# Token halves for the first and last batch, smaller mask products and a moved residual in a transformer kernel on one core

## What is computed

```python
x = x + L0_xattn(layernorm(x), ctx, ctx)   # 16 heads of width 8, softmax over 77 keys
# two layers on y = layernorm(x):
y = y + local_attention(rotary(l2norm(q), l2norm(k)), v) @ wo    # 8 heads of 64, windows of 64
h = layernorm(shift_token(y)) @ w1 + b1
y = y + (a * gelu(g)) @ w2 + b2                                  # a, g = the halves of h
x = x + y
x = x + softmax(layernorm(x) @ ctx + bias) @ ctx @ w_out         # second cross attention
# last feed-forward on z = layernorm(x), activations rounded to integers:
scale = 127.0 / max(abs(z)); q = clip(round(z * scale), -128.0, 127.0) / scale
x = x + bitlinear(gelu(bitlinear(z)))                            # both products use such rounded q
```

## Time and profile before

| | before |
|---|---|
| median of 3 runs | 757.89 us |
| lowest, highest | 753.37, 759.18 us |
| profiled execution: its time, its span | 759.17, 757.4 us |
| PE busy | 620.7 us, 82% |
| DVE busy | 558.1 us, 74% |
| ACT busy | 441.3 us, 58% |
| POOL busy | 238.4 us, 31% |
| mean granted TensorE clock | 0.934 of full speed |

### The profile page before, as it was taken

How to read it: one execution, slowest core, us unless ns; L and a number is a source line. 1 busy time by engine, 2 the same in 40 slices (tenths; PEclk the granted TensorE clock), 3 DMA queues, 4 the chain that set the end, 5 groups by cost and what they waited for, 6 DMA issues and landing times.

```text
span 757.4 us, 16460 instructions
## 1 busy us (share of the span) xinstructions
PE 620.7 (82%) x6368; PEld 424.3 (56%) x6368; DVE 558.1 (74%) x1344; ACT 441.3 (58%) x1083; POOL 238.4 (31%) x153
## 2 busy tenths in 40 slices
PE   5888877879899987688797899849889998899833
PEld 3565544557555763464564656626557676576621
DVE  3829877795878665855756877688787658979986
ACT  2233413674597668278567578557865963952814
POOL 2001221441224423334345135431443423503420
PEclk9899977998999999899999999959999999999975
DMA  8380001000200010020020020001102000000000
GB/s 223 102 183 1 2 0 37 13 3 2 50 1 2 21 31 1 1 49 1 2 49 1 2 48 2 2 0 29 36 2 49 2 2 1 2 1 15 2 15 14
DMA packets 27993, 19.00 MB, mean 25 GB/s; under 512 B 14894, under 2 KB 23692, under 8 KB 27916
## 3 DMA queue, kind: packets, MB, share of 16 engines
q1 hardware_dynamic: 27196, 17.82, 9.9%
q10 hardware_dynamic: 720, 0.13, 0.1%
HBM read 9.56 MB, written 1.05 MB: 14 GB/s over the span
## 4 chain that ended last, share of the span: by engine, by line
PE 45%; DVE 25%; ACT 14%; issue 8%; SPq 4%; POOL 2%; DMA 1%; DVEq 0%; POOLq 0%; ACTq 0%
PE ps L830 6%; PE ps L759 5%; ACT probs_l L1047 4%; PE ps L895 3%; SPq L571 3%; PE ps L710 3%; PE ps L855 3%; PE ps L867 3%; PE ps L918 3%; PE ps L744 3%; PE ps L842 2%; PE ps L885 2%; ACT squares L1030 2%; DVE rot_b L1358 2%; PE ps L925 2%
## 5 line engine op out<-in xcount | busy, mean ns | idle before, releaser
L650 POOL TENSOR_TENSOR probs_l<-probs_l,row_sum_l 128x1024 f32<-128x1024 f32 x32 | 64.2, 2005 | 130.3 <-DVE row_sum_l L1386 120.6
L643 POOL TENSOR_TENSOR rot_a<-rot_a,rot_b 128x1024 f32<-128x1024 f32 x32 | 76.6, 2398 | 74.4 <-DVE rot_b L1358 74.4
L1047 ACT ACTIVATE probs_l<-ps,neg_max_l 128x128 f32<-128x128 f32 x256 | 90.3, 378 | 13.3 <-DVE neg_max_l L1378 13.1
L830 PE MATMUL ps<-wqkv,hT_l 128*128 128x512 f32 x128 | 72.0, 645 | 17.9 <-DVE rot_b L1358 16.6
L1357 DVE TENSOR_TENSOR rot_a<-ps,rot 128x512 f32<-128x512 f32 x64 | 44.0, 687 | 53.4 <-ACT squares L1030 47.3
L1030 ACT ACTIVATE squares<-ps 128x512 f32<-128x512 f32 x64 | 38.7, 604 | 64.2 <-PE ps L830 62.7
L710 PE MATMUL ps<-k_diag,hT 32*128 32x308 f32 x256 | 57.6, 489 | 13.5 <-DVE probs L1225 8.9
L991 ACT ACTIVATE probsT<-ps 128x512 f32<-128x512 f32 (+1 forms) x96 | 47.7, 528 | 31.2 <-PE ps L744 30.9
L980 ACT ACTIVATE probs<-probs 128x1232 f32<-128x1232 f32 x32 | 39.4, 1236 | 35.3 <-DVE probs L1225 22.8
L918 PE MATMUL ps<-hT_f,w 128*128 128x512 f32 x96 | 52.8, 632 | 7.0 <-ACT gelu_g L1080 3.9
L1047 ACT ACTIVATION_READ_ACCUMULATOR probs_l<-ps,neg_max_l 128x1 f32 x256 | 55.7, 218 | 0.0
(11 more groups left out here) (169 smaller groups left out, 1463.9 us busy)
## 6 DMA issues: line engine op xcount, KB each, us to landing
v_win<-v_win SPq DMA_DIRECT2D x56, 128.0 KB, 2.3
score_bias<-fside_1x16xSxS SPq DMA_DIRECT2D x4, 616.0 KB, 8.3
wqkv<-L_ffn_wqkv SPq DMA_DIRECT2D x2, 768.0 KB
x_res<-x SPq DMA_DIRECT2D x4, 256.0 KB
w<-L_ffn_w SPq DMA_DIRECT2D x6, 128.0 KB
out<-x_res SPq DMA_DIRECT2D x3, 256.0 KB, 2.5
rot_a<-L_ffn_w SPq DMA_DIRECT2D x2, 256.0 KB, 4.0
probs_l<-c_rot SPq DMA_DIRECT2D x1, 512.0 KB
```

The source lines that it names most:

```text
L643: g.tensor_tensor(rot_a[:, t], rot_a[:, t], rot_b[:, t % 2], ALU.add).then_inc(rot_added.sem, 1)
L650: g.tensor_tensor(w, w, row_sum_l[:, t].unsqueeze(2).to_broadcast([P, LH, P]), ALU.mult).then_inc(probs_ready.sem, 1)
L830: mm(to, hl[:, tile(t)], wqkv[:, l, k * INNER:(k + 1) * INNER], start=True, stop=True).then_inc(ps.fill(it, "QK", t, k), 1)
L1047: last = a(probs_l[:, t % 2, tile(hd)], ps.bank(it, "S", t, half)[:, tile(c)], ACT.Exp, bias=neg_max_l[:, t, hd:hd + 1], accum_out=row_sum ...
```

## The change

1. `parts` also cuts A0, the first batch's first cross attention, into two halves of two tiles. Norm statistics, root, normalised tiles, transposition and query product now follow the parts as well, for A0 and C3 (for C3 there is no query product). The second half's queries come behind the scores of the first tile. The last product, the feed norm and the start of the projection of block (0,0) come in halves too.
2. The last product of block (3,1), the last batch's last layer, comes in two halves, each added and signalled alone (`ffn_parts`).
3. SP loads batch 1 ahead of the last two weights of the feed-forward and the 51 loads of L571.
4. The rotary tables are made as the last step of the weight preparation, ahead of the last tile's scores of A0, and no longer at the start of the projection.
5. The mask is added by four products of 64x64 weights and 512 columns, each at its own quarter of the array.
6. In layer 1 POOL adds y to x once y holds the bias, and DVE adds the product directly to x: one addition of DVE where there were two.
7. The clip in `to_integers` is gone.
8. ORDER has new rows for all five engines. Of K there are 130 steps as before.

```diff
-    return ((0, 1), (2, 3)) if it is CROSS[-1] else (tuple(range(TILES)),)
+    return ((0, 1), (2, 3)) if it in (CROSS[0], CROSS[-1]) else (tuple(range(TILES)),)
+def proj_parts(it):
+    return parts(AT["A", it.batch, None]) if it.index == 0 else (tuple(range(TILES)),)
+def ffn_parts(it):
+    return parts(AT["C", it.batch, None]) if it.layer == LAYERS - 1 else (tuple(range(TILES)),)
...
     "sync":
-        "Z4 U26 Z1 U6 Z2 W1 Z1",
+        "Z5 U32 Z3 W1 Z1",
...
# SP
                 for dst, src in o_loads:
                     sp.dma_start(dst, src).then_inc(o_in, 16)
+                load_x(1)
                 for dst, src in wd_loads:
                     sp.dma_start(dst, src).then_inc(wd_in, 16)
...
-                for b in batches[1:]:
+                for b in batches[2:]:
                     load_x(b)
...
# POOL, ffn_units
                 g.tensor_tensor(yb, yb, b2_row[:, l].unsqueeze(1).to_broadcast([P, TILES, D]), ALU.add).then_inc(plus_ready_l.sem, 1)
+                if l:
+                    xb = x[:, it.batch]
+                    pool.wait_ge(*plus_ready_l(it))
+                    g.tensor_tensor(xb, xb, yb, ALU.add).then_inc(x_plus_ready.sem, 1)
...
# PE, score_units
-                    masked = mask[:, min(t, 1)].unsqueeze(1).to_broadcast([P, CH, P])
-                    for half in halves:
-                        mm(to[half].rearrange("p (c k) -> p c k", c=CH), ident_b, masked, start=True, stop=False, skip_group_check=True)
+                    for j in halves:
+                        for half, heads in enumerate((lo, hi)):
+                            masked = mask[heads, min(2 * t + j, 1)].unsqueeze(1).to_broadcast([WIN, CH, P])
+                            mm(to[half][j * WIN:(j + 1) * WIN].rearrange("p (c k) -> p c k", c=CH), ident_b[heads, heads], masked,
+                               start=True, stop=False, tile_position=(WIN * half, WIN * j), skip_group_check=True)
...
# DVE, to_integers
-                for t in some:
-                    last = v.tensor_scalar(tmp[:, t], tmp[:, t], 127.0, -128.0, ALU.min, ALU.max)
-                step(last)
...
# DVE, weight_units (and taken out of proj_units)
                 v.tensor_copy(wt2.rearrange("p c d -> p (c d)"), turned[:, F:2 * F]).then_inc(ps.empty(it, "wturn"), 1)
                 yield
+                rotary_tables()
+                yield
...
# DVE, cross_units (the normalised tiles h and the queries follow the same loop)
-                statistics("X", spread_ready["X"], xb)
-                yield
+                for n, some in enumerate(parts(it)):
...
+                    statistics("X", spread_ready["X"], xb, some)
+                    yield
...
# DVE, ffn_units
-                dve.wait_ge(*ps.full(it, "Z"))
-                dve.wait_ge(*plus_ready_l(it))
-                v.tensor_tensor(yb, yb, four(ps.bank(it, "Z")), ALU.add).then_inc(ps.empty(it, "Z"), 1)
...
-                    v.tensor_tensor(x[:, it.batch], x[:, it.batch], yb, ALU.add).then_inc(x2_ready.sem, 1)
-                yield
+                for n, some in enumerate(ffn_parts(it)):
+                    dve.wait_ge(*ps.full(it, "Z", n))
+                    dve.wait_ge(*(x_plus_ready(it) if l else plus_ready_l(it)))
+                    to = (x[:, it.batch] if l else yb)[:, some[0]:some[-1] + 1]
+                    v.tensor_tensor(to, to, four(ps.bank(it, "Z", n))[:, 0:len(some)], ALU.add).then_inc(ps.empty(it, "Z", n), 1)
+                    dve.wait_ge(*ps.drained(it, "Z", n))
+                    dve.sem_inc((x2_ready if l else y_ffn).sem, 1)
+                    yield
```

More of the change, by code:

```diff
@@ L81, in cross_groups @@
             if t == 0:
+                for n in range(1, len(parts(it))):
+                    yield from queries(it, n)
                 yield from ((it, ("VF", n), 1) for n in range(len(CHUNKS)))
@@ L92, in cross_groups @@
             if after.stage == "A":
-                yield from queries(after)
+                yield from queries(after, 0)
         yield it, ("O", TILES - 2), 1
@@ L121, in ffn_groups @@
     yield from ((("F", c, k), 1) for c in range(HC) for k in range(2))
-    yield ("Z",), 1
+    yield from ((("Z", n), 1) for n in range(len(ffn_parts(it))))
 def attention_groups():
@@ L767, in feed_units @@
                 it, part, some = feed
-                if it.index == 0:
+                if it.index == 0 and part == 0:
                     pe.wait_ge(o_in, 16 * len(o_loads))
@@ L819, in proj_units @@
                     pe.wait_ge(pads_zeroed, 3)
-                pe.wait_ge(*(y_ffn(AT["F", it.batch, 0]) if l else block_in_ready(AT["A", it.batch, None])))
-                to = opens(it, "xT")
-                for t in tiles:
-                    last = tr(to[:, tile(t)], yb[:, t], ident)
-                last.then_inc(ps.fill(it, "xT"), 1)
-                yield
-                pe.wait_ge(*ps.drained(it, "xT"))
-                for t in tiles:
-                    for k in halves:
-                        to = opens(it, "QK", t, k)
-                        mm(to, hl[:, tile(t)], wqkv[:, l, k * INNER:(k + 1) * INNER], start=True, stop=True).then_inc(ps.fill(it, "QK", t, k), 1)
-                        yield
+                for n, some in enumerate(proj_parts(it)):
+                    pe.wait_ge(*(y_ffn(AT["F", it.batch, 0]) if l else block_in_ready(AT["A", it.batch, None], n)))
+                    to = opens(it, "xT", n)
+                    for t in some:
+                        last = tr(to[:, tile(t - some[0])], yb[:, t], ident)
+                    last.then_inc(ps.fill(it, "xT", n), 1)
+                    yield
+                    pe.wait_ge(*ps.drained(it, "xT", n))
+                    for t in some:
+                        for k in halves:
+                            to = opens(it, "QK", t, k)
+                            mm(to, hl[:, tile(t)], wqkv[:, l, k * INNER:(k + 1) * INNER], start=True, stop=True).then_inc(ps.fill(it, "QK", t, k), 1)
+                            yield
             def score_units(it):
@@ L921, in ffn_units @@
                     pe.wait_ge(*ps.drained(it, "F", c, 1))
-                to = opens(it, "Z")
-                for t in tiles:
-                    for c in range(HC):
-                        last = mm(to[:, tile(t)], gated[:, c, tile(t)], w2[:, l, c], start=(c == 0), stop=(c == HC - 1))
-                last.then_inc(ps.fill(it, "Z"), 1)
-                yield
+                for n, some in enumerate(ffn_parts(it)):
+                    to = opens(it, "Z", n)
+                    for t in some:
+                        for c in range(HC):
+                            last = mm(to[:, tile(t - some[0])], gated[:, c, tile(t)], w2[:, l, c], start=(c == 0), stop=(c == HC - 1))
+                    last.then_inc(ps.fill(it, "Z", n), 1)
+                    yield
             def warm_units(w):
@@ L1286, in feed_units @@
                 if it.stage == "A":
-                    normalise("Z", root_ready[stream](feed, 0), y[:, it.batch % RING], xb).then_inc(block_in_ready.sem, 1)
+                    normalise("Z", root_ready[stream](feed, 0), y[:, it.batch % RING], xb, some).then_inc(block_in_ready.sem, 1)
                     yield
```

196 lines of the change are left out of this document (107 added, 89 removed), and 83 rows, old and new, of the table ORDER.

## The result

| | before | after |
|---|---|---|
| median of 20 runs each | 755.84 us | 752.55 us |
| lowest, highest | 753.24, 759.18 | 748.18, 755.97 |
| ratio, 95% interval | | 0.9948 [0.9933, 0.9963] |
| profiled execution: its time, its span | 759.17, 757.4 | 751.38, 749.5 |

The change makes the kernel 0.5% faster, 3.9 us by the ratio, where 740 us was forecast and 730 to 752 given as the range. The median of 752.55 us lies just outside it. So the traces differ by 7.9 us, and about half of that is chance of the two executions. In what follows a sum of microseconds is a ratio times 755.7, and traces are used for where things lie.

The account below looks back on a forecast made before the run. PE was taken to bound the middle, where a saved microsecond counts about half, and DVE the last 118 us. Terms of 18.6 us off 759.2 gave 740.6, less 1.3 for the median 739.3, stated as 740 us, range 730 to 752.

Parts of the forecast that it names:

- Order: New table of steps for all engines: beyond the other terms no row can price it; taken as 0, 6 us either side.
- Rival (d): Late weights make the early tables hold DVE, or the order misfits: 5 us and 6 us lost, 755 us; chance 0.06.
- Early load, tables, halves of the first batch: Start of the run: DVE has more work behind it by A1's first scores; gain 4.5 us, ends 0 and 8.8.
- Masks: PE, 32 tiles: four overlapping masks save 0.21 us each, 6.7 us of PE, counted at half as 3.4 us.
- Rival (c): The four masks on PE don't overlap: 762 us, 781 at full weight, 750 if they merely stream; chance 0.07.
- Clips: DVE, integer feeds: 2.3 us less per batch; 4.6 us in full for the last two batches, 3.5 for the first two.
- Residual: Layer 1: four additions move from DVE to POOL; the three not counted in the halves into C3 gain 1.0 us.
- Halves into C3: End of block (3,1): DVE handles the first half while the second half's product runs; gain 1.6 us.

Follow-up runs that it names:

- e10: Kernel before with only the new order and the halves, every other edit undone: ratio 1.0086, 762.3 us.
- e9: Kernel before, old order, with three edits alone (clips gone, four 64x64 masks, batch 1 loaded early): ratio 0.9844, 743.9 us.
- e17: Changed kernel's order and halves with clips gone, 64x64 masks and early load, but residual on DVE and tables in the first projection: ratio 0.9917, 750.1 us.
- e5: Changed kernel with the rotary tables made in the first projection again: ratio to the kernel before 0.9938, 0.8 us faster than the changed kernel.
- e7: Kernel before with batch 1 loaded ahead of the weights, rotary tables where they were: ratio 0.9959, -3.1 us.
- e2: Kernel before with four 64x64 masks in place of two of 128x128: ratio 0.9950, -3.8 us.
- e1: Kernel before without the clip in to_integers, in all feeds: ratio 0.9938, -4.7 us.
- e3: Kernel before with y added to x on POOL in layer 1: ratio 1.0016, +1.2 us.
- e8: Changed kernel with y added to x on DVE again: ratio to the kernel before 0.9936, 0.9 us faster than the changed kernel.
- e18: Changed kernel, tables early, without 28 of the 40 early filler steps: ratio to the kernel before 0.9941, 0.5 us faster than the changed kernel.
- e11: Changed kernel without 28 of the 90 late filler steps, from 600 to 640 us: ratio to the kernel before 0.9968.
- e12: Changed kernel with tables in the first projection and without 28 of the 40 early filler steps: ratio to the kernel before 0.9901, 748.1 us.

## Why the prediction was wrong, step by step

**The step that failed is "Order": "I take 0, with 6 us to both sides".** Order and halves alone cost 6.5 us (e10), a little over the end of that margin, and 5.5 beside the three edits (e9, e17). The prediction said that no row could price the order, and then let it stand for nothing. The loss lies behind block (3,0), in two stretches that take some 5 us longer each; why they do is in part open. Rival (d), with a chance of 0.06, comes nearest: it had 6 us lost in the order and gave 755 us. Its other half did not happen as told. The weights came 1.3 us late and not several, and in the new order the early tables cost some 0.8 us (e5), not 5.

**Early load, tables, halves of the first batch, 4.5.** The load alone gives 3.1 (e7), and in the new order the early tables take 0.8 of it or nothing (e5). The end of the transfer was forecast for 35.4 to 40.7 us, and 39.4 was taken; it came at 40.7. Two small misses meet there: the last issue stood at 35.49 us and not at 34.95, and the bound of 40.7 counts the 5.3 us of its row from the end of an issue, while the row counts them from its start. h of A1 was done at 54.4 us (53.24 and 1.11) and not at 51.3: 1.3 us of the 3.1 are the transfer, and DVE also waited 2.1 us for A1's keys, which the forecast took as there. The first projection product did come sooner, at 71.9 us in place of 79.7, and the first mask later, as the scores that it overtook still had to be done. The halves of A0, which the prediction costs at nothing since they finish early, were not tried apart.

**Masks, 3.4.** Right: 3.8 (e2). PE saves 0.28 us a tile and not 0.21, and a little under half of that counts. That column tiling switches fast weight load off (the Trainium skill, TensorEngine Tiling, Restrictions and Gotchas) did not cancel it. The loads of 64x64 have a median of 103 ns, no less than the 98 ns of the 128x128 ones before. So a load of a quarter of the size is not cheaper here, in which the trace is at one with the rule; the 53 ns that the prediction estimated for one is about half of what was measured. But the four lie beside other work, and the scores still come 0.28 us sooner. Rival (c) is out.

**Clips, 4.6 and 3.5.** 4.7 in all (e1). The mechanism is right and the size is not. Of the last two batches 3.1 us came. In the trace of after the last feed, C3's, gave 2.4 us: 0.8 in its small clips and twice 0.8 in the large ones. C2's gave next to nothing: in the chain of waits, from h of C3 to the last output product of its scores it took 38.15 us before (682.48 to 720.63) and 37.85 after (677.03 to 714.88). Before, this stretch of the chain of waits ends with DVE:

```profile
718.96 0.77 DVE hidden L1130 x2
...
719.75 0.44 DVE int_d L1133
...
720.24 0.40 PE ps L803 x4
```

After, it goes through ACT, whose exponentials of C3 come behind C2's activations and behind 1.28 us of loading a table for them:

```profile
708.77 1.28 ACT L1017
...
710.07 1.24 ACT probs L1017
...
711.35 0.67 PE ps L775 x4
```

A DVE busy for 90% of the time was not the only limit: 2.3 us of work taken from it gave 0.3 us here. For the first two batches the rest of e1's 4.7 is left, 1.6 us of 3.5.

**Residual, 1.0.** No gain came: e3 gives a loss of 1.2 us whose interval still touches none, and e8 points the same way. The addition did leave the path: from the start of block (3,1)'s last product to h of C3 it took 7.05 us before (675.43 to 682.48), 6.43 in e3. What took this back is not shown.

**Halves into C3, 1.6.** Mis-sized: 7.05 us become 6.58 with halves alone (e10), 0.5 us. The prediction let the second product run beside DVE's work on the first, but they share a bank: the two products last 3.7 us (670.72 to 674.44) where one lasted 2.94. The forecast of "some 72.7 us" from the product that ends block (3,1) to the end was 75.0, counted from the second product.

**The sum.** Forecast 18.6. The parts alone give 4.7 + 3.8 + 3.1 - 1.2 - 6.5 = 3.9, without the early tables and with the halves in the last term. The masks came near. The clips, read from rows too, gave 4.7 of 8.1. The term that no row could say was the one furthest off.

## What to carry to other kernels

In a kernel with a fixed table of steps, an edit and a new order are two changes: time the edits with the old order first. Here three edits gave 1.6%, and the new order alone lost 0.9%. Effects measured alone need not add up, so try the combinations before trusting a sum. Compare windows of two traces by the same place in the work, not by the same microsecond. Before moving an operation ahead of a wait, list what stands behind it on its engine and what the other engines were told to do meanwhile; filler work put there becomes a second wait, and taking away one alone may show nothing. What a saving on the fullest engine is worth is bounded by the chain through the next one, so follow that too before counting it in full.

## What the runs showed of the hardware

- Four mask products of 64x64 by 512 columns on four quarters of the array take 0.24 us to the first score product, the two of 128x128 took 0.52.
- A weight load of 64x64 in bf16 has a median of 103 ns, one of 128x128 98 ns.
- With 28 filler steps fewer from 600 to 640 us (6.2 us of products), the granted clock of that stretch and the next fell from 1.00 to 0.92 and 0.91 in the traced execution, and the block behind ended 4.9 us later. In five traces of the new order with these steps (after, e5, e10, e17, e18) it is 1.00 in both. But the old order, with as few filler products between the ends of (2,1) and (3,1) as e11 (50 and 48), keeps 1.00 there (before, e9), with PE busy for 51.8 of 58.6 us. Fewer fillers therefore need not cost clock.
- From 40 to 80 us the granted clock was 0.96 in after, 0.91 in e5 with all fillers, 0.91 in e12 and 0.83 in e18 with 28 fewer. It does not follow the fillers alone, and e12 was the fastest of the four.
- The last small load behind some 50 others took 5.2 us from issue to landing in after and a load of batch 1 5.3 us before.
